# Perceiver layer: P·V with small zero-padded V weights over normalised probabilities, and another step sequence

## The reference, cut to what matters

```python
x = x + xattn(layernorm(x), ctx, ...)        # scores are linear: no softmax
x = x + attn(layernorm(x), Wq, Wk, Wv, Wo)   # causal, window 64
x = x + ffn(layernorm(x), ...)

# both softmax attentions, per batch and head:
attn = softmax(scores, axis=-1)              # 64 x 64
out  = einsum('bhqk,bhkd->bhqd', attn, v)    # d = 16
out  = out.transpose(0, 2, 1, 3).reshape(B, S, D) @ Wo
```

## Time and profile before

| what | value |
|---|---|
| median of 3 runs | 269.38 us |
| the profiled execution's own time | 269.51 us |
| its span | 267.7 us |
| PE busy | 243.5 us, 91% |
| PE weight loads | 217.0 us, 81% |
| DVE busy | 177.8 us, 66% |
| ACT busy | 119.2 us, 45% |
| POOL busy | 69.4 us, 26% |
| chain that ended last | PE 74%, DVE 8%, ACT 7% |

### The profile page before, as it was taken

One profiled execution on the slowest core, in us unless ns is written; L12 is line 12 of the kernel. 1 busy time (PEld: TensorE's weight loads), 2 busy tenths in 40 slices (PEclk: granted clock), 3 DMA queues, 4 the chain that ended last, 5 costly groups with the idle time before them and its releaser, 6 DMA issues.

```text
span 267.7 us, 4160 instructions
## 1 busy us (share of the span) xinstructions
PE 243.5 (91%) x1562; PEld 217.0 (81%) x1562; DVE 177.8 (66%) x376; ACT 119.2 (45%) x205; POOL 69.4 (26%) x74
## 2 busy tenths in 40 slices
PE   1988989999989999988977999999889989999991
PEld 2978989998979999777966998787658968998880
DVE  2545882696984997477767486997378556348463
ACT  4525745435175372273714599761363214541000
POOL 4011120212123023011661343797400010340010
PEclk9999999999999999999997999999999999999999
DMA  6999768775534020200020002252000000000010
GB/s 200 394 396 402 232 176 307 240 254 157 169 90 155 2 73 5 82 0 0 4 78 0 2 0 80 81 142 94 0 2 0 0 0 2 0 2 0 21 39 20
DMA packets 8851, 26.11 MB, mean 98 GB/s; under 512 B 1400, under 2 KB 3200, under 8 KB 8576
## 3 DMA queue, kind: packets, MB, share of 16 engines
q1 hardware_dynamic: 8832, 25.86, 28.6%
HBM read 25.33 MB, written 0.52 MB: 97 GB/s over the span
## 4 chain that ended last, share of the span: by engine, by line
PE 74%; DVE 8%; ACT 7%; issue 6%; DMA 2%; SPq 1%; POOL 1%; POOLq 0%; DVEq 0%; ACTq 0%
PE ps L627 68%; PE ps L630 6%; DMA raw<-in_ctx 2%; DVE prob L1137 1%; SPq L353 1%; POOL rstd L408 1%; DVE mx L1136 1%; DVE Z L950 1%; ACT prob L550 1%; DVE on L1149 1%; ACT raw L478 1%; ACT L611 1%; ACT kblk L542 1%; DVE kblk L1191 1%; ACT L598 0%
## 5 line engine op out<-in xcount | busy, mean ns | idle before, releaser
L627 PE MATMUL ps<-ch 128*128 128x130 f32 (+1 forms) x208 | 53.6, 274 | 5.5 <-ACT ch L507 5.4
L627 PE MATMUL ps<-ch,cl 128*128 128x260 f32 (+1 forms) x208 | 53.3, 317 | 0.0
L627 PE MATMUL ps<-w,hT 128*128 128x512 f32 x192 | 47.3, 401 | 0.0
L627 PEld LDWEIGHTS ps<-ch 128*128 128x128 f32 (+1 forms) x208 | 41.2, 198 | 6.3 <-ACT ch L507 5.3
L627 PEld LDWEIGHTS ps<-w,hT 128*128 128x128 f32 x192 | 35.7, 188 | 8.9 <-issue 0.5
L627 PEld LDWEIGHTS ps<-ch,cl 128*128 128x128 f32 (+1 forms) x208 | 41.0, 197 | 0.4 <-issue 0.2
L1051 DVE TENSOR_TENSOR cl<-raw,ch 128x1024 fp32r<-128x1024 f32 (+1 forms) x31 | 30.8, 1025 | 7.5 <-ACT ch L514 7.3
L514 ACT ACTIVATE ch<-raw 128x1024 fp32r<-128x1024 f32 (+1 forms) x31 | 26.3, 887 | 14.2 <-DMA raw<-in_ctx 8.3
L408 POOL TENSOR_TENSOR rstd<-ve,half_exp 128x2 f32<-128x2 f32 (+1 forms) x14 | 9.5, 678 | 78.3 <-DVE ve L922 78.2
L627 PE MATMUL ps<-xHL,dense 128*128 128x256 f32 x192 | 25.8, 295 | 1.5 <-DVE xHL L1200 1.5
L627 PEld LDWEIGHTS ps<-xHL,dense 128*128 128x128 f32 x192 | 24.8, 200 | 2.0 <-DVE xHL L1200 1.8
(11 more groups left out here) (162 smaller groups left out, 422.7 us busy)
## 6 DMA issues: line engine op xcount, KB each, us to landing
raw<-in_ctx SPq DMA_DIRECT2D x23, 512.0 KB, 4.3
raw<-in_w SPq DMA_DIRECT2D x8, 512.0 KB, 3.6
w<-in_w SPq DMA_DIRECT2D x2, 1024.0 KB, 9.8
stage<-in_dense SPq DMA_DIRECT2D x4, 512.0 KB, 5.8
mask<-in_mask SPq DMA_DIRECT2D x1, 800.5 KB, 9.2
rows<-in_rows SPq DMA_DIRECT2D x1, 768.0 KB, 7.9
raw<-in_ctx SPq DMA_DIRECT2D x8, 65.0 KB
raw<-in_ctx SPq DMA_DIRECT2D x4, 128.0 KB, 2.5
```

What stands on the lines that cost most here:

```text
L627: return pe.matmul(o, l, r, start=start, stop=stop, skip_group_check=not check)
```

## The change

The probabilities are now divided by their row sums before they are turned: the step `sums` becomes `shares`, with one DVE operation more over all 1024 columns, and PE's `turn_p` waits for `shares` instead of for the exponential. In `values` the operands change places: V is the stationary operand, as 64 keys by 32 columns, of which 16 hold one head's values and 16 are zero (`vz`), and `probT` moves, 64 keys by 64 queries. Two such products, one for each head of a pair, add up in one place of PSUM, on 32 partitions. There are 32 of them for a tile, over 8 places (4 strips of 32 output partitions, 2 banks and halves of the key partitions). The result is already transposed, so that ACT copies it to `aT`; DVE's `values`, `turn_o` on both engines and the parity masks there go. And the four lists of steps are other ones.

```diff
+            def padded_values(bank):
+
+                got = ps[:, bank, :].rearrange("p (c h d) -> p c h d", h=2, d=HD)
+                for hl in range(2):
+                    last = act.activation(vz[:, :, :, hl, hl * HD:(hl + 1) * HD].rearrange("p t c d -> p (t c) d"),
+                                          got[:, :, hl, :], ACT.Copy)
...
+                elif step == "values":
+                    act.wait_ge(sem("pv"), i + 1)
+                    copy(aT[i % 2][:, :, :, :].rearrange("p j b q -> p b j q"),
+                         ps[:, tile_bank(i):tile_bank(i) + 2, 0:P].rearrange("p b (j q) -> p b j q", j=KC), "aT")
...
-                    pe.wait_ge(sem("prob"), i + 1)
+                    pe.wait_ge(sem("shares"), i + 1)
...
-                    for c in range(H // 2):
-                        last = mm(ps[:, tile_bank(i), c * 4 * HD:(c + 1) * 4 * HD], probT[:, i % 2, c, :],
-                                  vblk[:, i % 2, c, :, :].rearrange("p b d -> p (b d)"), True, True)
+                    spots = [(r, bb) for r in range(4) for bb in range(2)]
+                    for j in range(KC):
+                        for hl in range(2):
+                            for r, bb in spots:
+                                keys = slice(bb * S, bb * S + S)
+                                last = mm(ps[32 * r:32 * r + 32, tile_bank(i) + bb, j * S:(j + 1) * S], vz[keys, i % 2, 4 * j + r, hl, :],
+                                          probT[keys, i % 2, 4 * j + r, hl * S:(hl + 1) * S], hl == 0, hl == 1)
...
-                elif step == "turn_o":
-                    pe.wait_ge(sem("on"), i + 1)
...
-                elif step == "sums":
+                elif step == "shares":
...
-                    link(dve.tensor_reduce(sm[:, k, :], prob[:, k, :, :].rearrange("p c (b k) -> p (c b) k", b=2), AX.X, ALU.add))
+                    link(dve.tensor_reduce(sm[:, k, :], rows_of, AX.X, ALU.add))
                     link(dve.reciprocal(rs[:, k, :], sm[:, k, :]))
...
-                elif step == "values":
...
-                elif step == "turn_o":
...
+                    dve.tensor_tensor(rows_of, rows_of, rs[:, k, :].unsqueeze(2).to_broadcast([P, H, S]),
+                                      ALU.mult).then_inc(sem("shares"), 1)
...
-        ("score_product", 6), ("experts", (0, 3)), ("score", 6), ("score_product", 7), ("experts_product", (1, 0)),
...
+        ("experts", (0, 3)), ("score_product", 6), ("score", 6), ("shares", 6), ("experts_product", (1, 0)),
...
```

More of the change, by code:

```diff
@@ L106, in first_half_steps @@
     return [
[L107 to L110, removed]
-        ("score", 1), ("cross2_product", 5), ("sums", 0), ("cross2", 5), ("split", 22), ("turn_p", 1), ("sums", 1),
@@ new lines, in first_half_steps @@
+        ("split", 18), ("turn_z", (0, 0)), ("split", 19), ("piece", 0), ("cross2", 4), ("piece", 1),
+        ("proj1_product", 0), ("proj1", 0), ("score_product", 0), ("score", 0), ("cross3", 4), ("gram", 17),
+        ("cross4", 4), ("shares", 0), ("evac", 5), ("score_product", 1), ("gram", 18), ("turn_p", 0), ("score", 1),
+        ("cross1", 5), ("gram", 19), ("shares", 1), ("split", 20), ("cross2_product", 5), ("turn_p", 1),
+        ("values", 0), ("values", 1), ("cross2", 5), ("project", 0), ("project", 1), ("norm2", 0), ("cross3", 5),
@@ new lines, in first_half_steps @@
+        ("split", 21), ("split", 22), ("gram", 20), ("evac", 6), ("turn_z", (0, 1)), ("split", 23), ("cross4", 5),
+        ("cross1", 6), ("proj2", 0), ("piece", 2), ("gram", 21), ("cross2_product", 6), ("piece", 3),
+        ("score_product", 2), ("cross2", 6), ("score", 2), ("cross3", 6), ("shares", 2), ("gram", 22),
+        ("score_product", 3), ("gram", 23), ("evac", 7), ("cross4", 6), ("turn_p", 2), ("score", 3), ("cross1", 7),
+        ("cross2_product", 7), ("shares", 3), ("turn_p", 3), ("values", 2), ("cross2", 7), ("values", 3),
@@ L121, in first_half_steps @@
+        ("project", 2), ("piece", 4), ("cross3", 7), ("project", 3), ("cross4", 7), ("xo_product", 1), ("rms1", 0),
+        ("turn_x", 0), ("hidden_product", 0), ("xo", 1), ("hidden", 0),
     ]
@@ L137, in second_half_steps @@
-        ("turn_p", 6), ("score", 7), ("experts_product", (1, 1)), ("sums", 6), ("turn_p", 7), ("sums", 7),
-        ("experts", (1, 0)), ("values", 6), ("values", 7), ("turn_o", 6), ("turn_o", 7), ("project", 6),
-        ("project", 7), ("experts_product", (1, 2)), ("rms1", 1), ("experts", (1, 1)), ("experts", (1, 2)),
-        ("turn_x", 1), ("experts_product", (1, 3)),
+        ("norm1", 1), ("hidden_product", 1), ("gates", 0), ("gate_groups", 0), ("hidden_product", 2),
+        ("hidden_product", 3), ("turn_z", (1, 0)), ("piece", 5), ("piece", 6), ("hidden_product", 4), ("hidden", 1),
@@ L141, in second_half_steps @@
+        ("shares", 7), ("turn_p", 7), ("values", 6), ("values", 7), ("experts", (1, 0)), ("project", 6),
+        ("project", 7), ("experts_product", (1, 3)), ("rms1", 1), ("experts", (1, 1)), ("experts", (1, 2)),
+        ("turn_x", 1),
     ]
@@ L227, in layer @@
     kblk, _ = place("kblk", [P, KC * BH, 4, S])
-    vblk, _ = place("vblk", [P, TH, H // 2, 2, 2 * HD])
+    vz, _ = place("vz", [P, TH, H // 2, 2, 2 * HD])
     prob, _ = place("prob", [P, TH, H // 2, 2 * S])
-    on = [place(f"on{k}", [P, 2, KC, 4, 2 * HD], at=where["prob"] + k * 4096)[0] for k in range(TH)]
     aT = [place(f"aT{k}", [P, KC, 2, S], at=where["prob"] + k * 4096 + 2048)[0] for k in range(TH)]
```

98 lines of the change are left out of this document (33 added, 65 removed).

## The result

| | before | after |
|---|---|---|
| median of the timed runs, us | 269.43 (269.06 to 269.57) | 279.97 (279.48 to 280.92) |
| profiled execution, its span | 269.51, 267.7 | 280.92, 279.1 |
| PE, DVE busy in the span, us | 243.5, 177.8 | 239.3, 176.3 |

A forecast was written before the change was run, and what follows sets the result against it. PE, busy 243.5 of 267.7 us, was taken as the bound. PE work of -8.0 us and waits of +11.5 made +3.5 on 269.51, so 273.0 us, with a range from 264 to 281.

The forecast's parts named there:

- D's second turn: Pair D, RoPE attention of the second half: PE waits 2.1 us for the divided probabilities before the second tile's turn.
- C's second: Pair C, second half: PE waits another 1.0 us at the second tile's turn, DVE's division ending at 181.0.
- A's: Pair A, first half, with Gram chunks as cover: PE waits 1.1 us at the second turn.
- B's: Pair B, first half: PE waits 0.2 us at the turn, after 1.4 for `cross1` 7.
- C's first turn: Pair C, first tile: `shares` ends at 173.4, so PE waits 2.9 us in place of 0.5.
- Rival 1: Narrow `values` products: strips don't overlap or a 25 to 27 ns floor holds; 3.4 us a pair, 276.7 us; chance 0.22.
- rival 2: Narrow `values` products: a narrow load costs what a wide one does; 7.1 us a pair, 290.4 us; chance 0.10.
- PE's work falls by 8.0: All four pairs: 4.4 us of PE work removed and 2.4 added, 2.0 us less per pair, 8.0 in all.
- Opening, the dense steps between, and the closing list: nothing: Steps outside the pairs: same work in nearly the same order, covered by PE's backlog, set at nothing.
- nothing stands between now: End of pair D: no expert product between turn and second half's first dense product, 2.2 us later; it comes at 225.3.
- a cost on top: Lower PE clock, 1.2 GHz: more waits at D's end could bring a second such stretch, 1.7 us, outside the sum.
- Rival 3: Second turn of each pair: the longer way is hidden, kernel faster; 265.3 us with two thirds hidden; chance 0.28.

The follow-up runs named there:

- the old-then-new run: Change's operations without the division, before's list up to the first half's turn of x, the change's list from there: 270.76 us, 1.004 to before.
- the two spliced runs: Change's operations without the division, lists exchanged at the first half's turn of x: new list then old 262.69 us, old then new 270.76 us.

## Why the prediction was right and where it failed

**Direction, and the waits for the division: right.** The kernel is slower, and the division on the way is the largest cost. At D's second turn PE waits 1.84 us (forecast 2.1), at C's second 0.74 (1.0), at A's 1.17 (1.1), at B's 0.38 (0.2). At C's first turn, where I had 2.9, PE came too late to wait, since hT had held it for 3.5; with that wait moved away it waited 5.0 there. Taken out, the division gives 4.9 us in the first half, where 4.9 of waits stood in the sum (the match is closer than the 1.5 us to which a place is known), and 4.1 in C and D, where 6.6 stood.

**The narrow products: 2.4 us a pair, measured 1.75**, near the lower bound. Rival 1 (3.4 us) and rival 2 (7.1) are refuted: the strips do overlap, and a narrow load is not paid like a wide one. The products came out 2.6 us cheaper over four pairs than they stood in the sum, so this step can't explain the loss.

By place, the forecast is 7.6 us short (11.1 for 3.5): 3.1 up to the first half's first dense product, 1.6 in C and D, and 2.9 behind them. Three steps failed.

**"PE's work falls by 8.0", counted in full: the first step that failed.** With 1.75 it fell by 10.6 (4 times 4.4 - 1.75), and in before's own list with no division it brought 5.1. In the first half 5.3 us less work brought 0.9 (and nothing by the place in the old-then-new run), where 4.0 stood in the sum. That is the 3.1: pairs A and B are bound by the way through score, exponential, turn and norm, and PE's work there lay beside it. (That it was beside another way is shown; that it was this one is read from the waits, and no run separates it.) I had added up PE's work and the waits as if each microsecond of the first was on the path. Only in C and D was it (4.2 of 5.3).

**"Opening, the dense steps between, and the closing list: nothing": the second.** For the opening and the first half the two spliced runs show no cost, and the closing steps cost nothing beside the clock. The list between them, behind the first half's turn of x, costs 4.3 us in C and D by the places, and some 6 us or more with the clock behind it. Two waits stand there that the runs with the old list don't have: 3.5 for hT, and 2.2 for xHL ahead of the second half's dense part. That they are the cost is read from the traces; the only moves against one of them put it off. In C and D the list's 4.3 is partly hidden in the total, since the waits for the division were 2.5 less than I had set. The wait for xHL I had seen ("nothing stands between now") and reckoned in D's chain. The wait for hT I missed by counting the steps ahead of a wait on PE alone: the pieces moved on ACT and POOL, and POOL's 2.4 us each went into its queue ahead of the hidden rows. That POOL was busy for 26% said nothing of this one stretch.

**The low clock, "a cost on top" of 1.7 us, outside the sum: the third.** It is a term. Up to the last matmul the lower clock held 10 us longer than before (13.7 for 3.4), and all of it, taken back, gave 2 to 3 us: the 2.9 behind the second half's first dense product.

**Rival 3** (hidden, faster) failed at its condition: pair D's `shares` did not end ahead of PE. **The range** held the time with 1 us to spare, for a reason that was not mine: it was drawn for 3.4 us a pair, and the list and the clock filled it.

So: -5.1 for the products (forecast -8.0), +10.2 for the division with the clock behind it (+11.5 with all waits), +6.0 for the list (0).

Open: how the costs divide between list and division to better than 3 us, what the waits for hT and xHL are worth if both are taken away, and whether the division in halves beats the kernel before when the old list stands behind the first half.

## What to carry to other kernels

Work taken from the busiest engine is worth its full time only in stretches where that engine runs without a wait; elsewhere price it at what the side way leaves. When a step moves in a list, follow it on each engine that it issues to: a piece that costs PE nothing took 2.4 us of POOL, ahead of what PE needed next. A wait of 2 us on PE can have a second price in the clock behind it, and where two late ways run side by side, take both away before you judge either.

## What the runs showed of the hardware

128 records of 64x32 weights and 64 columns, spread over both row halves and all four strips, took 1.75 us, 13.7 ns each, where a 128-column record takes 110. The Trainium skill (TensorE: Matmul & The Clock Gate, "Wait — 56ns, not 53.3ns?") puts the least distance between matmul starts at some 25 ns, by which 128 records would be 3.2 us, an estimate. The measurement decides: the floor does not hold when neighbouring records lie in different row halves and strips. At D, where part of the stretch was at the lower clock, the same records took 2.07.

VectorE's reciprocal costs 6.3 ns a column, and a multiplication of the same 256 columns 0.42 us in all. And the four products of 64 columns with 128x128 weights that bring the reciprocals into place took 1.08 us a tile (8 records, at full clock), as much as the eight turns of a whole tile of probabilities (1.09), which have twice the columns: there the wide load is paid, 193 ns in the median as in the earlier trace rows, and not the columns.

The lower clock doesn't follow every wait. The wait for xHL in the first half is 1.54 us in both kernels; before has 3.4 us at the lower clock behind it, and after has none. The one of 2.21 us in the second half is followed by 6.8 us of it in after, by 3.4 without the division, and by none with the division in halves.
